# A transformer tower with tree-routed experts on one core: residual adds one tile ahead of their scatters, the zeros of a weight table in five parts, slot arithmetic over two units

## The reference, cut to what matters

```python
h = conv1d(sign(x), sign(kernel)) + bias ...        # x: (4, 750, 128), three taps -> h: (4, 748, 64), batch norm
h = h + attention(layernorm(h))                     # 8 heads of 64, softmax over 748 x 748 scores, its diagonal weighs v
z = layernorm(h).reshape(2992, 64)
node = 0
for level in range(8):                              # a binary tree of 255 nodes
    score = z . w1s[node] + b1s[node]
    y    += gelu(|score|) * (z @ w2s[node] + b2s[node])
    node  = 2 * node + (score > 0) + 1
out = h + y
```

## Time and profile before

| | |
|---|---|
| median of 3 runs | 474.11 us |
| the profiled execution | 474.62 us, its span 472.7 us |
| busy share of the span | PE 75%, VectorE 72%, ScalarE 69%, GpSimd 60% |
| attention, units 0 to 15 | to about 318 us |
| last slots, scatters, reloading of rows | about 318 to 365 us |
| tree, 32 static and 12 overflow tiles | about 365 us to the end |
| GpSimd, residual add of a tile (L723) x44 | 328 ns median |
| GpSimd, scatter of a tile (L726) x44 | 44.7 us busy, 35.1 us idle before them |

### The profile page before, as it was taken

One profiled execution on the slowest core, in us unless ns is written; L12 is line 12 of the kernel. 1 busy time (PEld: TensorE's weight loads), 2 busy tenths in 40 slices (PEclk: granted clock), 3 DMA queues, 4 the chain that ended last, 5 costly groups with the idle time before them and its releaser, 6 DMA issues.

```text
span 472.7 us, 8346 instructions
## 1 busy us (share of the span) xinstructions
PE 352.7 (75%) x2606; PEld 248.5 (53%) x2606; DVE 342.5 (72%) x577; ACT 324.0 (69%) x832; POOL 284.2 (60%) x398
## 2 busy tenths in 40 slices
PE   1156896878789889777898769883512999999970
PEld 1144565655456555445664446552312777788860
DVE  0475969899788878998888998978530789955440
ACT  1363996788888998577898656758200799987760
POOL 4315748786867875584689662661552365666663
PEclk9996999989999999989999999995555999999995
DMA  4425243417998972131243130018915012120000
GB/s 95 128 62 136 53 113 81 101 39 172 178 187 160 151 182 47 53 97 29 71 113 97 38 82 1 3 42 116 118 31 139 23 36 56 33 54 6 12 15 5
DMA packets 58953, 37.27 MB, mean 79 GB/s; under 512 B 31661, under 2 KB 57607, under 8 KB 58906
## 3 DMA queue, kind: packets, MB, share of 16 engines
q1 hardware_dynamic: 54778, 33.81, 35.7%
q0 software_dynamic: 3328, 2.36, 2.0%
q10 hardware_dynamic: 800, 0.49, 0.5%
HBM read 11.42 MB, written 7.50 MB: 40 GB/s over the span
## 4 chain that ended last, share of the span: by engine, by line
DVE 33%; issue 17%; ACT 15%; PE 15%; POOL 12%; DMA 5%; SPq 1%; POOLq 0%; DVEq 0%; ACTq 0%
DVE nm L1392 14%; ACT Z L1192 10%; POOL out L726 8%; PE Z L923 6%; POOL pre L723 3%; DMA pre<-in_x 3%; DVE va L1421 2%; ACT q L1134 2%; DVE pre L1488 2%; ACT k L1134 1%; PE Z L843 1%; DMA pool_a<-pool_a 1%; DVE pre L1503 1%; DVE va L1437 1%; DVE pre L1665 1%
## 5 line engine op out<-in xcount | busy, mean ns | idle before, releaser
L1192 ACT ACTIVATE Z<-Z,nm 125x748 f32<-125x748 f32 x192 | 166.3, 872 | 61.5 <-DVE nm L1392 60.2
L1392 DVE TENSOR_REDUCE nm<-Z 125x1 f32<-125x748 f32 x192 | 175.4, 933 | 36.4 <-PE Z L923 30.0
L923 PE MATMUL Z<-pool_a 128*125 128x512 f16 (+1 forms) x768 | 162.0, 338 | 28.1 <-ACT Z L1192 23.4
L923 PEld LDWEIGHTS Z<-pool_a 128*125 128x125 f16 x768 | 87.7, 140 | 71.8 <-ACT Z L1192 46.0
L726 POOL DMA_INDIRECT out<-pre,va x44 | 44.7, 1017 | 35.1 <-POOL pre L723 35.1
L1665 DVE TENSOR_REDUCE pre<-va 128x64 f32<-128x512 f32 x44 | 45.7, 1039 | 5.8 <-ACT va L1275 2.4
L790 PE MATMUL Z<-xhT,wq 128*128 128x249 f16 (+1 forms) x192 | 32.9, 291 | 11.9 <-DVEq L1402 10.5
L1192 ACT ACTIVATION_READ_ACCUMULATOR Z<-Z,nm 125x1 f32 x192 | 41.2, 215 | 0.0
L652 POOL DMA_INDIRECT sorted_rows<-xrow,slot x24 | 30.4, 1266 | 15.3 <-DVE slot L1544 8.7
L620 POOL TENSOR_TENSOR va<-va 125x256 f32<-125x256 f32 (+2 forms) x54 | 29.6, 548 | 10.3 <-DVE va L1421 7.2
L596 POOL TENSOR_TENSOR pool_a<-q,pool_a 128x748 f16<-128x748 f32 x15 | 24.7, 1644 | 10.2 <-DVE pool_a L1349 9.1
(11 more groups left out here) (243 smaller groups left out, 667.1 us busy)
## 6 DMA issues: line engine op xcount, KB each, us to landing
pool_a<-pool_a SPq DMA_DIRECT2D x64, 187.0 KB, 3.3
pool_a<-pool_a SPq DMA_DIRECT2D x64, 93.5 KB, 2.2
sorted_rows<-zrow SPq DMA_DIRECT2D x1, 3640.0 KB, 23.8
va<-sorted_rows SPq DMA_DIRECT2D x12, 260.0 KB, 3.0
w<-in_L_ffn_w2s SPq DMA_DIRECT2D x1, 2048.0 KB, 16.5
pre<-in_x SPq DMA_DIRECT2D x4, 375.0 KB
pool_a<-in_L_ffn_w2s SPq DMA_DIRECT2D x1, 1024.0 KB
out<-pre,va POOLq DMA_INDIRECT x44, 2.2
```

The source lines that it names most:

```text
L923: last = mm(z[0:XP, c0:c1], kst[:, u % 3, a, hd, KST[t]:KST[t] + XP], qst[:, u % 3, hd, c0:c1], start=(a == 0), stop=(a == 1))
L1192: sc_.activation(z, z, ACT.Exp, bias=nm[0:XP, u % 4, i:i + 1], accum_out=sm[0:XP, u % 4, i:i + 1]).then_inc(s_exp, 1)
L1392: v.tensor_reduce(nm[0:XP, u % 4, i:i + 1], Z[n % 3][0:XP, 0:N], X, ALU.max, negate=True).then_inc(s_max, 1)
```

## The change: three edits

1. GpSimd adds the residual of tile k + 1 before it scatters tile k (static tiles). In the overflow tiles VectorE adds the residual itself, behind its sum.
2. The zeros of the leaf table are written in five parts of 64 x 1,664, one in each unit 5 to 9 behind the product of q and k. The copy of the leaf columns moves from u = 4 to u = 10, the load of the bias row from SyncE's unit 7 to 13.
3. The prefix sum and the rank product are cut into two halves of 375 tokens each. In the loop the halves of the prefix sum stand at (1,1) and (1,3), the counts at (1,5), the six small operations at (2,1), the rank halves at (2,3) and (2,5); `pf` goes from (1,10) to (2,7) and `sl` from (2,9) to (2,10).

```diff
@@ fills
-                f += {(0, 8): [("A", b - 1, 0)], (0, 10): [("A", b - 1, 1)], (1, 10): [("pf", b - 1)],
-                      (2, 9): [("sl", b - 1)]}.get((ph, i), [])
+                f += {(0, 8): [("A", b - 1, 0)], (0, 10): [("A", b - 1, 1)], (2, 7): [("pf", b - 1)],
+                      (2, 10): [("sl", b - 1)]}.get((ph, i), [])
+        ZERO_AT, ZPARTS = 5, 5
@@ SyncE
-                    sp.wait_ge(s_z7, 1)
+                if w == 13:
+                    sp.wait_ge(s_z7, ZPARTS)
                     sp.dma_start(w7[D:D + 1, :].rearrange("p (n o) -> p n o", o=E1)[:, :, 0:D],
@@ GpSimd
                 link(gp.memset(xrow[:, :, C_ONE:C_ONE + 1], 1.0))
-                link(gp.memset(w7[D:P, :], 0.0))
-                pool.sem_inc(s_z7, 1)
+            def leaf_zeros(n):
+                c = LEAVES * E1 // ZPARTS
+                gp.memset(w7[D:P, n * c:(n + 1) * c], 0.0).then_inc(s_z7, 1)
+                pool.wait_ge(s_z7, n + 1)
 ...
+                pool.wait_ge(s_z7, ZPARTS)
                 link(gp.tensor_copy(w1_columns(w7, slice(0, LEAVES)), w1T[:, LEAVES - 1:NODES]))
 ...
-                if u == 4:
+                if ZERO_AT <= u < ZERO_AT + ZPARTS:
+                    pool.wait_ge(s_prod, u + AHEAD + 1)
+                    leaf_zeros(u - ZERO_AT)
+                if u == ZERO_AT + ZPARTS:
                     leaf_columns()
 ...
-            def rows_out(k):
+            def residual(k):
                 pool.wait_ge(s_sl, k + 1)
                 o = yo[:, k % NO, :]
                 gp.tensor_tensor(o, o, xs[:, (k // 4) % NX, k % 4, C_H:C_ID], ALU.add).then_inc(s_yo, 1)
-                pool.wait_ge(s_yo, k + 1)
+            def rows_out(k):
+                if k < ST_TILES:
+                    pool.wait_ge(s_yo, k + 1)
+                else:
+                    pool.wait_ge(s_yov, k - ST_TILES + 1)
 ...
+            residual(0)
             for k in range(ST_TILES):
+                if k + 1 < ST_TILES:
+                    residual(k + 1)
                 rows_out(k)
@@ TensorE, slots
-                pe.wait_ge(s_xt, b + 1)
+                pe.wait_ge(s_xt, 2 * (b + 1))
@@ VectorE
-                link(v.tensor_tensor_scan(Ct, ones[:, 0:1].to_broadcast([P, NIN]), mT, zrow[:, 0:1], ALU.mult, ALU.add))
+                scan(0)
+            def scan(n):
+                half_ = slice(n * TH, (n + 1) * TH)
+                link(v.tensor_tensor_scan(Ct[:, half_], ones[:, 0:1].to_broadcast([P, TH]), mT[:, half_],
+                                          Ct[:, TH - 1:TH] if n else zrow[:, 0:1], ALU.mult, ALU.add))
 ...
-            def rank_of_token(b):
-                v.tensor_tensor(Xt, Ct, mT, ALU.mult).then_inc(s_xt, 1)
+            def rank_of_token(b, n):
+                half_ = slice(n * TH, (n + 1) * TH)
+                v.tensor_tensor(Xt[:, half_], Ct[:, half_], mT[:, half_], ALU.mult).then_inc(s_xt, 1)
+            def old_terms():
                 v.tensor_scalar(col[:, c_cap], col[:, c_grp], float(G), float(G + 1), ALU.mult, ALU.add)
 ...
-                    if 1 <= b < B - 1 and (ph, i) == (1, 1):
-                        leaf_ranks(b - 1)
-                    if 1 <= b < B - 1 and (ph, i) == (1, 3):
-                        leaf_counts(b - 1)
-                    if 1 <= b < B - 1 and (ph, i) == (1, 5):
-                        rank_of_token(b - 1)
+                    if 1 <= b < B - 1:
+                        if (ph, i) == (1, 1):
+                            leaf_ranks(b - 1)
+                        if (ph, i) == (1, 3):
+                            scan(1)
+                        if (ph, i) == (1, 5):
+                            leaf_counts(b - 1)
+                        if (ph, i) == (2, 1):
+                            old_terms()
+                        if (ph, i) in ((2, 3), (2, 5)):
+                            rank_of_token(b - 1, (i - 3) // 2)
 ...
+            def add_residual(k):
+                dve.wait_ge(s_sl, k + 1)
+                o = yo[:, k % NO, :]
+                v.tensor_tensor(o, o, xs[:, (k // 4) % NX, k % 4, C_H:C_ID], ALU.add).then_inc(s_yov, 1)
 ...
                         weigh(k)
                         sum_levels(k)
+                        add_residual(k)
```

More of the change, by code:

```diff
@@ L220, in tower @@
             "slots", "ln2_rstd", "w1_columns")]
-        (s_b0, s_bnp, s_bn, s_bq8, s_z7, s_zl, s_abs, s_xp, s_xc, s_y, s_yv, s_y0, s_wa, s_wy, s_sl, s_yo) = [sem(n) for n in (
-            "b0_in", "bn_by_feature", "bn_ready", "q_bias_ready", "w7_zeros", "low_zeros", "gate_abs", "xs_T", "xsT_copied", "y_ready", "y_moved", "root_moved", "weighted_by_act", "weighted", "levels_summed", "rows_out")]
+        (s_b0, s_bnp, s_bn, s_bq8, s_z7, s_zl, s_abs, s_xp, s_xc, s_y, s_yv, s_y0, s_wa, s_wy, s_sl, s_yo, s_yov) = [sem(n) for n in (
+            "b0_in", "bn_by_feature", "bn_ready", "q_bias_ready", "w7_zeros", "low_zeros", "gate_abs", "xs_T", "xsT_copied", "y_ready", "y_moved", "root_moved", "weighted_by_act", "weighted", "levels_summed", "rows_out", "overflow_rows_out")]
         vs, ps_, as_ = sem("vector_step"), sem("pool_step"), sem("scalar_step")
@@ L271, in fills @@
             return f
+        ZERO_AT, ZPARTS = 5, 5
+        assert LEAVES * E1 % ZPARTS == 0
         CENTERED = {0: 1, 2: 2, 3: 3}
@@ L1630, in _ @@
                         ln2_last()
-                        rank_of_token(B - 2)
+                        for n in range(2):
+                            rank_of_token(B - 2, n)
+                        old_terms()
                     if u == NU and i == 9:
@@ L1635, in _ @@
                         leaf_ranks(B - 1)
+                        scan(1)
                         leaf_counts(B - 1)
-                        rank_of_token(B - 1)
+                        for n in range(2):
+                            rank_of_token(B - 1, n)
+                        old_terms()
             dve.wait_ge(s_lam, 1)
```

## The result

The changed kernel takes 486.16 us (median of 4 runs, 485.74 to 487.44), the kernel before, on the same chip, 474.75: a ratio of 1.025 with a 95% interval of 1.019 to 1.031. I had forecast 471.0 and gave a slower kernel 6 in 100. The profiled executions are 485.82 (span 484.3) and 474.62 (span 472.7).

The account below looks back on a forecast made before the run. GpSimd's scatters waiting for its own adds were taken to bound the end; in the attention three engines alternate as late one. -4.0 - 2.2 + 1.0 + 0.7 + 1.0 + 0.4 = -3.1, from 474.1 to 471.0 us; range 465.4 to 474.2.

Parts of the forecast that it names:

- the tail: End of the overflow tiles: last scatter starts at 461.8 instead of 465.79, -4.0 us, bounds -4.7 and -3.5.
- the fallback: Static tiles: if the 0.79 wait is not hidden, 12 scatters at 1.8 follow 440.1 and still reach 461.7.
- the splits of batches 2 and 3: Behind the loop: a prefix sum of 1.78 becomes two of about 0.97 with a wait, +0.2 each, +0.4.
- the counts' lock: Counts at (1,5), where GpSimd's casts and subtractions start: held 0 to +2.0 us a batch, taken as 1.4.
- the softmax weights: Softmax weights at i = 7 slip onto other GpSimd work: +0.3 us (-0.2 to +1.3).
- the rank half's lock: Unit 10, batch 0: second rank half meets GpSimd's cast or subtraction, 0 to 1.6 us, taken as 0.5.
- the group slots: Linked small operations, 2.1 us, moved to (2,8) beside the q and k product: 0 to +2.2, taken as 1.0; unit 14, 0.
- the wait for the zone of `yp`: Batch 1: `sl` waits until VectorE has weighed `yp` 8, scores of step 11 queued behind: +0.6 us (0 to 1.2).
- The small chains are torn apart: Rival, chance 0.08: units 9 and 13, counts last as long as GpSimd's stream, +6 each; 481 us.
- The other three rivals: Locks missed, 465.8 (0.24); unit 2's hold-up returns, 473.0 (0.18); static tiles gain less, end unmoved (no chance given).
- unit 2's hold-up: Rival, chance 0.18: ScalarE or a bank late where VectorE was, or unit 6 loses more; zeros net +0.8, 473.0 us.
- the locks: GpSimd holding VectorE's small operations through shared SBUF ports; rival that they are missed: both batches -3.5, 465.8 us, chance 0.24.

Follow-up runs that it names:

- the run that has that burst: Against the kernel before: VectorE adds the residuals of the overflow tiles, GpSimd's static tiles unchanged, no filling; 481.78 us, ratio 1.0125.
- the light pacing: Adds changed as in edit 1 only, plus small GpSimd fillings behind each scatter (128 columns static, 256 overflow), against the kernel before; 472.12 us, 0.9946; rerun 474.26, 0.9955.

## Why the prediction was wrong, point by point

**Edit 1, the tail: right in its term, wrong in its cover.** "-4.0 us, bounds -4.7 and -3.5" is -4.1 (6.17 to 2.06); VectorE's add 0.23 for 0.25; the static period mostly 1.49 to 1.61 for 1.57 between the pauses; the chain's end passed to VectorE as said. The step that failed is the one that had no number: I wrote that GpSimd "remains the slower one in the static tiles, but 0.57 us a tile less so" and took every sum's time as given. A scatter every 1.57 us beside the tree tiles is in no row of before; there they stand 2.14 apart. (Beside the attention six row scatters came, from 242.57 on, at periods of 1.78 and then 1.50 us, and no engine idled over 0.32 in them; that would have misled me too.) The runs give +6.7 static and +2.1 overflow in the changed kernel, 7.0 static with the edit alone. It should have been bounded as an unknown: the tiles beside it cost 46.5 us, and a range that left them untouched on both sides was too narrow. Even the fallback I wrote ("12 scatters without adds, at 1.8 ... would reach 461.7 too") names the burst. They came every 1.28, not every 1.8, and the run that has that burst lost 8.7 us in the overflow tiles, with 11.6 us in one period.
The Trainium skill, "SBUF — State Buffer", section "Who interferes with whom", says that TensorE and ScalarE never wait on anyone for SBUF, and that a DMA never contends with a compute engine. I had weighed only its lock between VectorE and GpSimd. In these runs the releases from TensorE to ScalarE are late where GpSimd scatters densely, and TensorE is busy 49.0 us out of 53.5, with a full clock, against 46.15 out of 46.15 with the light pacing. Whether through SBUF or another way no run shows; for the time, the measurement decides.

**Edit 2: right in both terms, wrong where it said nothing.** -2.25 for -2.2 in unit 2, +1.14 for +1.0 in unit 6, L1356 at 0.17. But "nothing" for units 5, 7, 8 and 9 fails: units 8 and 9 lose 0.3 and 0.5 with this edit alone. I had looked at what stands beside the zeros themselves, not at what GpSimd's later work, pushed back by 1.5 us, comes to stand beside.

**Edit 3: the sum missed at both batches.** Against the profiled execution before, units 8 to 10 are +4.1 for "+0.7 (-3 to +3.5)" (in the run with edit 3 alone +3.4), units 12 to 15 +3.3 for "+1.0 (-1.5 to +2.7)"; the splits of batches 2 and 3 +0.5 for +0.4. Term by term, batch 0: the counts' lock +0.8 for 1.4 (199.91, 0.97 where 0.15 was due), the softmax weights +0.4 for +0.3 (0.80 for 0.41), the rank half's lock 0 for 0.5, the group slots +2.0 for 1.0 (bound 2.2). Their sum, 3.2, is mine. A term is missing: the six small operations, moved to (2,1), take 1.4 us instead of 0.7, as two of them are held (211.58, 0.55, and 212.22, 0.43). What failed is that I let a lock cost its own length. Behind 4.06 us without a maximum, TensorE idled 2.52, and then came 10.2 us at 1.2 GHz, three scores of 1.22 fewer. The prediction has no word of TensorE's clock, though the profile's row of clock tenths has a 6 and two 8s in the attention. In unit 14 the group slots' lock was 0, as I took it (2.0 us in all), and the wait for the zone of `yp`, taken as 0.6, was one of 1.29 for TensorE; three stretches at 1.2 GHz lie in units 14 and 15 or begin there (from 287.2, 304.3 and 321.3). Such stretches occur there without edit 3 as well, so how much of the second batch is its own stays open: unit 14 takes 21.0 to 23.3 with group slots at (2,8) in five of the six kernels that have them there (18.7 in the sixth), and 18.0 to 22.0 in twelve profiles of kernels with the old slots.

**The rivals.** "The small chains are torn apart (0.08)" gave 481 and a slower kernel, as -4.8 for the rest and +12 for this; edit 3 alone cost 5.6 us (482.40 against 476.80). Its place was right (group slots and counts beside GpSimd's stream, decided from +4.8 on both batches: 7.5 was reached), its mechanism only half: two of the ten links of the group slots were held, not all, and most of the price was TensorE's idleness and clock (5.7 us in unit 10, of which the holds are 2.0). That its 481 comes as near as it does to 486.16 is luck: it has 12 for what cost 5.6 alone, and nothing of the tree's loss. The other three rivals did not occur: unit 2's hold-up stayed away, and the locks were met. No rival had the tree.

## What to carry to other kernels

When an edit makes a queue denser than any row of the trace shows it, its own saving is only one term: bound what its neighbours may lose, and try the same edit paced before dropping it. A held-up operation on the engine that feeds TensorE can cost more than its length: here holds of 2.0 us left TensorE idle for 2.52, and 10 us at 1.2 GHz followed. Work that is pushed back delays its queue, so check what that queue then stands beside. Move chains of small VectorE operations by where GpSimd's long operations end, not by which unit has idle time on average.

## What the runs showed that I had not expected

- Indirect scatters by GpSimd delayed TensorE's releases of ScalarE in the tree when they filled 63% of GpSimd's time or more (periods 1.28 to 1.5 us; 6.7 to 9.4 us lost over 31 tiles, 8 to 9 in a burst of eight or nine), and not at 49% or less. Half the rows per scatter changed nothing; plain writes from GpSimd at 1.46 us did no harm. The share alone does not decide: the six row scatters named above filled 79% and disturbed nothing, and in the changed kernel the first twelve scatters of the static tiles passed before the first pause. The loading of instructions alone does not explain the pauses: in the same 44 us (376 to 420) the DMA records have four blocks of 16 KB and four smaller ones both with edit 1 and with plain writes, and with plain writes nothing pauses. Which part of a scatter does it stays open, and scatters from another engine's queue were not tried.
- Stretches at 1.2 GHz come at other places from one kernel's profile to the next, where the work is the same. Unit 14 took 18.0 to 18.2 us in six profiles with the old slot arithmetic, 20.5 in five and 22.0 in one, and those six have such a stretch between 284 and 299. So a unit's time from a single profile can be 2.5 us off for this reason alone, once it was 4, and the 15.3 us of unit 10 before are the low end of twelve profiles (15.3 to 16.7).
